# State-space scan: the skip term and the gate on GpSimd, in place of an identity product on TensorE and a product on VectorE

## The reference, cut to what matters

```python
def step(h, inputs):
    dA_t, dt_t, B_t, x_t, C_t = inputs
    dBx = jnp.einsum('bh,bn,bhp->bhpn', dt_t, B_t, x_t)
    h = h * dA_t[:, :, None, None] + dBx
    y = jnp.einsum('bhpn,bn->bhp', h, C_t)
    return (h, y)
...
y = jnp.moveaxis(ys, 0, 1) + D[None, None, :, None] * x     # skip term
y = y.reshape(b, l, D_INNER)
y = rmsnorm(y * jax.nn.silu(z), ssm_norm_w)                 # gate
```

## Time and profile before

| what | value |
|---|---|
| median of 3 runs | 1815.76 us (1814.04 to 1816.18) |
| the profiled execution's own time | 1819.28 us |
| its span in the profile | 1817.5 us |
| busy share of the span: PE, DVE, ACT, POOL | 93%, 70%, 66%, 10% |
| granted PE clock, mean over the span | 0.962 of full speed |
| the stage of the change, rounds and tail | 1447.87 to 1541.74 us |
| POOL busy between 1434 and 1541.7 us | 0 |
| PE wait for DVE's gate product (L1549 for L1803), whole stage | 0.7 us, 2 times |
| DVE wait for PE's scores (L1769 for L1539), whole stage | 29.9 us, 5 times |

### The profile page before, as it was taken

How to read it: one execution, slowest core, us unless ns; L and a number is a source line. 1 busy time by engine, 2 the same in 40 slices (tenths; PEclk the granted TensorE clock), 3 DMA queues, 4 the chain that set the end, 5 groups by cost and what they waited for, 6 DMA issues and landing times. The chain is left out here.

```text
span 1817.5 us, 25943 instructions
## 1 busy us (share of the span) xinstructions
PE 1681.8 (93%) x10028; PEld 794.6 (44%) x10028; DVE 1268.1 (70%) x1804; ACT 1193.8 (66%) x2436; POOL 182.9 (10%) x171
## 2 busy tenths in 40 slices
PE   6999999999999999869999999999885798699997
PEld 3433333333333333245444444455553465344443
DVE  4888888888888888167788678574464366255555
ACT  4588888888888888845677777777546554333432
POOL 1000000000000000040000000111344000000100
PEclk9899999999999999989899999999988799699999
DMA  1000000000000000010000000000100000212220
GB/s 62 1 1 1 1 1 1 1 1 1 1 1 1 1 1 1 1 47 1 1 1 1 1 1 1 1 1 2 37 1 1 12 1 18 103 48 93 99 91 20
DMA packets 7274, 29.98 MB, mean 16 GB/s; under 512 B 680, under 2 KB 2736, under 8 KB 4848
## 3 DMA queue, kind: packets, MB, share of 16 engines
q1 hardware_dynamic: 7152, 28.33, 4.2%
HBM read 27.15 MB, written 1.18 MB: 16 GB/s over the span
## 5 line engine op out<-in xcount | busy, mean ns | idle before, releaser
L883 DVE TENSOR_REDUCE a_part_max<-a_ps 128x2 f32<-128x1024 f32 x512 | 602.5, 1221 | 86.9 <-PE a_ps L685 86.3
L868 ACT ACTIVATE a_probs<-a_ps 128x512 f32<-128x512 f32 x1024 | 533.1, 614 | 131.1 <-PE a_ps L781 128.6
L883 DVE TENSOR_REDUCE f_part_max<-f_ps 128x2 f32<-128x1024 f32 (+3 forms) x320 | 327.8, 1062 | 121.1 <-PE f_ps L685 65.2
L781 PE MATMUL a_ps<-a_q_shift,a_KA 64*128 64x512 f32 x1024 | 367.6, 448 | 3.6 <-POOL a_q_shift L664 2.4
L868 ACT ACTIVATE f_probs<-f_ps 128x512 f32<-128x512 f32 (+3 forms) x640 | 300.3, 539 | 99.8 <-PE f_ps L781 48.1
L781 PEld LDWEIGHTS a_ps<-a_q_shift,a_KA 64*128 64x128 f32 x1024 | 166.3, 187 | 290.8 <-ACT a_probs L868 275.1
L685 PE MATMUL a_ps<-a_KA,a_q_open 64*128 64x512 f32 x1024 | 278.0, 468 | 4.4 <-DVE a_part_max L883 3.8
L799 PE MATMUL a_psO<-a_probs,a_VA 128*32 128x512 f32 x2048 | 275.5, 610 | 3.9 <-ACT a_probs L868 3.9
L781 PE MATMUL f_ps<-f_q_shift,f_KA 64*128 64x512 f32 (+3 forms) x640 | 224.0, 435 | 4.7 <-POOL f_q_shift L664 2.2
L685 PE MATMUL f_ps<-f_KA,f_q_open 64*128 64x512 f32 (+3 forms) x640 | 170.4, 431 | 5.1 <-DVE f_part_max L883 4.3
L781 PEld LDWEIGHTS f_ps<-f_q_shift,f_KA 64*128 64x128 f32 x640 | 106.2, 188 | 150.1 <-ACT f_probs L868 138.4
(11 more groups left out here) (321 smaller groups left out, 1782.2 us busy)
## 6 DMA issues: line engine op xcount, KB each, us to landing
t_c_all<-c_rows SPq DMA_DIRECT2D x16, 1024.0 KB, 7.7
experts_w<-in_experts SPq DMA_DIRECT2D x1, 3264.0 KB, 10.5
W<-in_weights SPq DMA_DIRECT2D x1, 1574.0 KB, 6.2
out<-X SPq DMA_DIRECT2D x4, 256.0 KB, 6.8
K<-in_consts SPq DMA_DIRECT2D x1, 644.0 KB, 6.9
R<-in_rows SPq DMA_DIRECT2D x1, 530.0 KB, 5.9
W<-in_weights SPq DMA_DIRECT2D x1, 512.0 KB, 6.7
mx_conv_rows<-in_conv_rows SPq DMA_DIRECT2D x1, 512.0 KB, 3.5
```

Of the source, the lines that this page charges most:

```text
L781: mm = pe.matmul(bank(r)[:, lo:512], g.KA[rows, 2 * n + jp, P * s:P * s + P], q_shift[rows, u % 2, jp, lo:512], start=True, stop=not diag)
L868: nc.scalar.activation(probs[:, st % 2, j, lo:512], bank(r)[:, lo:512], ACT.Exp, scale=SCALE).then_inc(ring_read, 1)
L883: dve.tensor_reduce(part_max[:, 4 * q + 2 * jp:4 * q + 2 * jp + 2, c], ps1[:, k % 2, :, 0:b - a], AX_X, ALU.max).then_inc(max_read, 1)
```

## The change

The identity product is gone from PE: the four head products each start and end a bank region of their own. DVE's gate product is gone too. POOL, after the taps, now goes through the 16 chunks: it waits for DVE's sum (L1799), adds `skip` to it, waits for itself and multiplies by `z`, each on 128x256 f32 in SBUF, in place in `m.xs`. At the first chunk of each block it waits for the ring's last gate copy. PE's wait before a bank is reused is on DVE's sum instead of the product; ACT's wait before `skip` is overwritten is on POOL's addition. A semaphore is added.

```diff
--- before.py
+++ after.py
@@ -1447,6 +1447,7 @@
         d_ps, exp_done, sc_ps, gm_done, w_done = S_("d_ps"), S_("exp"), S_("scores_ps"), S_("gm"), S_("weights")
         cleared, carried, state_done = S_("state_cleared"), S_("carried"), S_("state")
         y_ps, y_scaled, y_sum, y_out = S_("y_ps"), S_("y_scaled"), S_("y_sum"), S_("y_out")
+        y_skip = S_("y_skip")
         ring = lambda k: ps[:, k % 2, :]
         d_bank = lambda c: ps[:, 2 + c % 2, :]
         s_bank = lambda c: ps[:, 4 + c % 2, :]
@@ -1466,6 +1467,15 @@
                 pool.wait_ge(rows_in, 16)
                 pool.tensor_tensor(taps[:], rows[:], g.w("mxbc")[:, 0:DI].unsqueeze(1).to_broadcast([P, CONV, DI]),
                                    ALU.mult).then_inc(taps_in, 1)
+                for c in range(C):
+                    n, i = c // 4, c % 4
+                    y = m.xs[:, c, :]
+                    if i == 0:
+                        pool.wait_ge(ring_read, ITEMS * n + Z1 + 1)
+                    pool.wait_ge(y_sum, c + 1)
+                    pool.tensor_tensor(y, y, skip[:, n % 2, i, :], ALU.add).then_inc(y_skip, 1)
+                    pool.wait_ge(y_skip, c + 1)
+                    pool.tensor_tensor(y, y, z[:, n % 2, i, :], ALU.mult).then_inc(y_out, 1)
 
             @block.tensor
             def _(pe):
@@ -1544,14 +1554,12 @@
 
                     n, i = c // 4, c % 4
                     if c >= 2:
-                        pe.wait_ge(y_out, c - 1)
-                    pe.wait_ge(ring_read, ITEMS * n + T_X1 + 1)
-                    pe.matmul(y_bank(c)[:, 0:DI], g.k("ident"), skip[:, n % 2, i, :], start=True, stop=False)
+                        pe.wait_ge(y_sum, c - 1)
                     pe.wait_ge(w_done, c + 1)
                     pe.wait_ge(xd_done, 2 * n + 2)
                     for h in range(MH):
                         pe.matmul(y_bank(c)[:, HD * h:HD * h + HD], seg[:, c % 8, h, :],
-                                  xd[:, n % 2, i, HD * h:HD * h + HD], start=False, stop=(h == MH - 1))
+                                  xd[:, n % 2, i, HD * h:HD * h + HD], start=True, stop=True)
                     if c:
                         pe.wait_ge(state_done, c)
                     else:
@@ -1630,7 +1638,7 @@
                     k = ITEMS * n + (T_X0, T_X1)[x]
                     act.wait_ge(xd_done, 2 * n + x + 1)
                     if n >= 2:
-                        act.wait_ge(y_ps, 4 * (n - 2) + 4)
+                        act.wait_ge(y_skip, 4 * (n - 2) + 4)
                     for h in range(2):
                         src = ring(k).rearrange("p (t c) -> p t c", c=P)[:, :, HD * h:HD * h + HD]
                         at = 2 * x + h
@@ -1797,10 +1805,6 @@
                                       over_cols(decay[:, 0, c, :], HD), ALU.mult).then_inc(y_scaled, 1)
                     dve.wait_ge(y_scaled, c + 1)
                     dve.tensor_tensor(y, y, y_bank(c)[:, 0:DI], ALU.add).then_inc(y_sum, 1)
-                    dve.wait_ge(y_sum, c + 1)
-                    if i % 2 == 0:
-                        dve.wait_ge(ring_read, ITEMS * n + (Z0, Z1)[i // 2] + 1)
-                    dve.tensor_tensor(y, y, z[:, n % 2, i, :], ALU.mult).then_inc(y_out, 1)
 
                 raw, one_more, log, gap = small[:, 0], small[:, 1], small[:, 2], small[:, 3]
                 dve.memset(states[:, 0, :], 0.0).then_inc(cleared, 1)
```

## The result

The changed kernel takes 1825.13 us (median of 6 runs, 1821.14 to 1826.36), the kernel before 1815.27 us beside it (6 runs, 1814.04 to 1816.18): a ratio of 1.0050, with an interval of 1.0038 to 1.0062. It is slower, by more than the forecast of 1819.1 and outside its range. In a second session the changed kernel came to 1825.45 us (12 runs) and the kernel before to 1819.15 us (35 runs); the medians are 6.3 us apart there, and the ratio on record is 1.0045.

What follows compares the result with a forecast made beforehand. PE was taken to bound the blocks, DVE the tail. Blocks +1.3, tail +0.9 and POOL's last operations +1.2 gave +3.4 us, +3.3 without rounding: 1819.1 us for the median, range 1811.5 to 1822.5.

Steps and rivals of the forecast that it cites:

- The hidden cost: POOL stops DVE: In each chunk, POOL's SBUF reads make DVE's weights 0.43 us late and the carry 0.95 in all; 0.50 net.
- rival 3: POOL's two operations per chunk cost 0.84 us each instead of 0.73; +5.6 us, 1821.4; chance 0.20.
- Rival 2: No stops that matter, POOL's and DVE's reads miss each other; blocks of 25.6 us; -4.0 us, 1811.7; chance 0.13.
- Rival 1: DVE keeps its turn, only the weights are late, 0.43 against 0.45 saved per chunk; -0.7 us, 1815.1; chance 0.20.
- Beside these, small: In the thinner tail the granted clock could fall, making the last chunk's products some 1.5 us longer; outside the sum.
- the bound: Limit between "same" and "slower": 0.2%, 3.6 us, about what a measurement of this kernel can tell from no change.

Runs made afterwards that it cites:

- the kernel with only the blocks filled: The changed kernel plus three PE products that nobody reads in each block, ahead of those waiting for ACT, none in the tail; 1821.82 us, 1.0021.
- both on DVE: The changed kernel with the skip addition and the gate product moved from POOL to DVE, nothing else different; 1825.19 us, 1.0031.
- the third filler kernel: The changed kernel plus PE products that nobody reads only in the tail: chunks 13 to 15, and two behind the last chunk; 1826.92 us, 1.0050.

## Why the prediction was wrong

**The stops: right.** "The hidden cost: POOL stops DVE" forecast weights at about 1.1, carries at about 1.0, POOL's product longer than its addition and a wait of PE of over 3 us. They are 1.11 to 1.19, 0.94, 1.05 against 0.73, and 3.65. POOL's operation is 0.73 by the line between the two sizes of the earlier trace rows, and rival 3's 0.84 fell; the Trainium skill (GPSIMD Engine Reference, Engine selection) puts such work at about twice VectorE's time, an estimate of 0.84 from the 0.42, and the rows give 0.73 to 0.42, a ratio of 1.7. Rival 2 fell with the first stop. Rival 1 fell with the carries: POOL's product gets in although DVE's next operation stands right behind the last.

**The blocks and the tail, without the clock: close.** Forecast, against the kernel before: −0.6, +0.93, +0.93 and +2.1; measured −0.57, +1.13, and, with PE's waits filled, +1.12 and +2.2. The sum is +3.9 against +3.3. The mis-sized term is the step from one chunk's sum to the next. "The hidden cost" puts a chunk's net loss at 0.50 us, but the sum carries 0.45 (3.42 for 2.97 in the tail; chunk 4's sum at 1486.37, which is 0.45 late). Measured, the steps of the chunks that are stopped grow by 0.49 (2.97 to 3.46) and, behind the first sum of each block, by 0.56 (2.97 to 3.53). POOL starts 0.08 us after DVE's sum, as assumed, except behind those first sums, where it starts 0.14 to 0.15 after (1486.22 to 1486.37). (In rival 2, 3 x 3 x 0.43 is 3.87 and not 3.84, which changes nothing.)

**The clock: the step that failed.** It is the one that begins "Beside these, small": the granted clock "could fall to its other level in the thinner tail", some 1.5 us, and was left out of the sum. The tail's part was sized well: 16.81 less 15.46 is 1.35 us. But it belonged in the sum, and block 2 was not thought of at all: 28.94 less 28.01, 0.9 us. The prediction had itself forecast PE's wait to grow from 0.8 to over 3 us and read from it only DVE's lateness, not what a PE that stands for 3.6 us does to the clock behind it. With these two, +2.3, the stage is +6.16 us instead of the forecast's +3.3.

**The next stage: costed at nothing.** Its work didn't change, but its length goes with the clock of its first 18 us. At 0.50 to 0.54 the rest takes 274.4 to 275.7 us, at 0.63 to 0.72 273.0 to 273.5, at 0.81 271.8 to 271.9, over thirteen profiles. Both profiles of the changed kernel have 0.50 and 275.2. The kernel before had 0.53, 0.54 and 0.81. Its profile of 1819.28 us has 0.53, so between the two profiles this costs nothing (6.16 in the stage, 0.36 in the lead-in, −0.5 in the rest: 6.0, the difference of the spans). Against the profile with 0.81 (1814.01 us) the spans are 11.2 us apart: 1.7 before the stage, 6.1 in it and 3.4 behind it. The medians' 9.9 us lie between these two cases, but no run divides them. That the six runs of before mostly had the higher clock there is inferred from their times (1814.04 to 1816.18); it wasn't seen in a profile of each. In the second session, where the median of before is 1819.15, the medians are 6.3 us apart, about what the stage alone gives. So the stage's +6.16 is shown as the cost of the change, and what lies beyond it isn't. That the change lowers the next stage's clock isn't shown either: the kernel before, whose tail ran at 1.00 each time, had 0.53 or 0.54 in two profiles of three, and the kernel with only the blocks filled, whose tail ran at 0.76, had 0.65.

**The chances.** "Slower" had 0.38 and "same" 0.50 because the forecast lay 0.3 us inside the bound. The clock's two terms of the stage, which the prediction had half in its hands, would have carried the forecast over it: 1819.1 + 2.3 = 1821.4, where the bound is 1819.4.

**What stays open.** Which of two equal waits the fall of the clock follows (in block 2 in the changed kernel and with both on DVE, in block 1 with the tail filled) isn't explained by PE's own rows, which are alike in blocks 1 and 2. That filling keeps it up is shown for the tail (fillers 1.00, none 0.71 to 0.76) and, for the blocks, as far as none of four filled waits was followed by a fall and four of eight unfilled ones were; what decides the place is not shown, nor what sets the clock at the start of the next stage. For the same reason the third filler kernel's time can't be split into its parts.

## What to carry to other kernels

Work moved to GpSimd is not free while it is "hidden": where both read SBUF, price each meeting with a two-input VectorE operation at the full wait (0.5 us for 128x256 here) and set it against what VectorE saves, or hold GpSimd back until VectorE works from PSUM, which, with the tail divided anew, turned +0.45% into −0.38%. When an edit makes another engine late, look at how long TensorE then stands, and price the products behind that wait at the lower clock too. And before forecasting against a profile, see how the one execution stands to the median, and in which stage the difference lies.

## What the runs showed of the hardware that was not expected

- A wait of 3.2 to 3.7 us of PE, in a block where it is busy 85% of the time (23.68 of 28.02 us), was followed by a fall of the granted clock in one block and not in the next: the wait of 3.65 us in block 1 of the changed kernel cost no clock, that of 3.64 in block 2 did.
- The clock of the next stage's start varies between executions of the same kernel (0.53, 0.54 and 0.81), and the rest of the span with it (275.7, 274.8 and 271.8 us), though the tail before it ran at 1.00 in all three.
- GpSimd's fills of 748 columns (0.72 us) beside two-input VectorE operations cost neither side anything, while two reads of 256 columns cost VectorE 1.02 us a chunk.
- With two inputs in SBUF on both sides, the engine that waited takes its turn although the other's next operation stands ready: carry 0.94, then POOL's product 1.05, in alternation.
